# The second layer's routing: router weights as the standing operand, logits turned once, ranks from a scan and two short products

## What is computed

```python
def _L1_ffn_ref(x, w1s, w2s, w3s, W1, W2, W3, Wg):
    xf = x.reshape(-1, C)
    shared = geglu(xf, w1s, w2s, w3s)          # every token
    logits = xf @ Wg                           # 128 x 8
    idx = jnp.argmax(logits, axis=-1)          # one expert for a token
    final = jnp.zeros_like(xf)
    for e in range(N_EXPERTS):
        y = geglu(xf, W1[e], W2[e], W3[e])
        final = final + jnp.where((idx == e)[:, None], y, 0.0)
    return (shared + final).reshape(B, T, C)

x = x + 0.5 * _L0_ffn_ref(...); x = x + _L0_attn_ref(...); x = x + 0.5 * _L0_ffn_ref(...)
x = x + 0.5 * _L1_ffn_ref(_layernorm(x), ...)
x = x + _L1_attn_ref(_layernorm(x), ...)
x = x + 0.5 * _L1_ffn_ref(_layernorm(x), ...)
```

## Time and profile before

| | |
|---|---|
| median of 3 runs | 1867.86 us (1866.92 to 1868.22) |
| span of the profiled execution | 1918.1 us; the profile gives no other time of that execution |
| TensorE busy | 1729.9 us, 90% of the span |
| VectorE, ScalarE, GpSimd busy | 67%, 58%, 63% |
| granted TensorE clock, mean | 0.971 of full |

### The profile page before, as it was taken

One profiled execution on the slowest core, in us unless ns is written; L12 is line 12 of the kernel. 1 busy time (PEld: TensorE's weight loads), 2 busy tenths in 40 slices (PEclk: granted clock), 3 DMA queues, 4 the chain that ended last, 5 costly groups with the idle time before them and its releaser, 6 DMA issues. The chain is left out here.

```text
span 1918.1 us, 35727 instructions
## 1 busy us (share of the span) xinstructions
PE 1729.9 (90%) x12089; PEld 1502.7 (78%) x12089; DVE 1279.6 (67%) x2981; ACT 1105.3 (58%) x1953; POOL 1210.5 (63%) x1201
## 2 busy tenths in 40 slices
PE   7998998999999899976779988899899999988889
PEld 6887776778878688765668867777899999877777
DVE  2358988888888987889894355334576766554333
ACT  3476766667676576756655452433677777542332
POOL 4248787787868778798985243565455555444554
PEclk9999999999999999998989999999899999989999
DMA  5023433323333233232224110113544554001113
GB/s 147 1 85 104 114 100 101 95 94 105 96 110 97 86 104 108 98 89 84 94 61 118 32 37 29 45 43 104 159 130 120 148 157 124 2 33 33 42 43 104
DMA packets 121486, 166.74 MB, mean 87 GB/s; under 512 B 14710, under 2 KB 56732, under 8 KB 121308
## 3 DMA queue, kind: packets, MB, share of 16 engines
q1 hardware_dynamic: 114268, 148.86, 25.7%
q0 software_dynamic: 7040, 15.60, 2.6%
HBM read 114.20 MB, written 50.20 MB: 86 GB/s over the span
## 5 line engine op out<-in xcount | busy, mean ns | idle before, releaser
L833 POOL TENSOR_TENSOR db<-du_m,bt 128x512 f32<-128x512 f32 x256 | 329.3, 1288 | 116.7 <-DVE bank L838 115.9
L838 DVE TENSOR_TENSOR_SCAN bank<-bank,db 128x512 f32<-128x512 f32 x256 | 312.6, 1221 | 18.2 <-ACT bank L823 17.7
L864 POOL TENSOR_TENSOR y_m<-y_m,ph 128x512 f32<-128x512 f32 x240 | 312.8, 1303 | 2.0 <-DVE ph L853 2.0
L823 ACT ACTIVATE bank<-dt_m,a_neg 128x512 f32<-128x512 f32 x256 | 176.3, 689 | 85.7 <-DVE ph L853 78.9
L853 DVE TENSOR_TENSOR ph<-bank,ct 128x512 f32<-128x512 f32 x240 | 165.9, 691 | 9.4 <-POOL y_m L864 1.1
L1355 POOL TENSOR_TENSOR s_a<-s_a,mx_a 128x768 f32<-128x768 f32 x64 | 94.1, 1470 | 87.1 <-DVE mx_a L1438 87.0
L1469 PE MATMUL bank<-vb_a,pT_a 96*128 96x64 f32 x1024 | 121.7, 272 | 0.0
L1469 PEld LDWEIGHTS bank<-vb_a,pT_a 96*128 96x128 f32 x1024 | 119.8, 193 | 0.0
L375 PEld LDWEIGHTS bank<-dn,hf1b 128*128 128x128 f32 x680 | 90.2, 194 | 16.1 <-DVE x_all L437 6.8
L375 PEld LDWEIGHTS bank<-dn,hf2b 128*128 128x128 f32 x680 | 90.2, 195 | 16.0 <-DVE x_all L437 8.3
L375 PEld LDWEIGHTS bank<-dn,hf0b 128*128 128x128 f32 x688 | 90.4, 193 | 12.0 <-DVE x_all L437 2.8
(11 more groups left out here) (480 smaller groups left out, 4877.1 us busy)
## 6 DMA issues: line engine op xcount, KB each, us to landing
bt<-bc_rows SPq DMA_DIRECT2D x128, 256.0 KB, 3.4
ct<-bc_rows SPq DMA_DIRECT2D x128, 256.0 KB, 3.4
sorted<-zero_row SPq DMA_DIRECT2D x64, 288.0 KB, 4.0
k_strips_a<-k_rows SPq DMA_DIRECT2D x32, 256.0 KB, 3.0
q_strips_a<-q_rows SPq DMA_DIRECT2D x32, 256.0 KB, 4.0
q_rows<-q_hi_a SPq DMA_DIRECT2D x16, 256.0 KB, 3.0
q_rows<-q_lo_a SPq DMA_DIRECT2D x16, 256.0 KB, 3.3
k_rows<-k_hi_a SPq DMA_DIRECT2D x16, 256.0 KB, 3.2
```

Of the source, the lines that this page charges most:

```text
L823: eng.activation(DH[J % 2][:], dt[s % 2][:, j % NH, :], ACT.Exp, scale=a_neg[:, j % NH, j // NH:j // NH + 1]).then_inc(da_done.sem)
L833: eng.tensor_tensor(db[J % RD][:], du[s % 2][:, j % NH, :], bt[N % RB][:], ALU.mult).then_inc(db_done.sem)
L838: eng.tensor_tensor_scan(DH[J % 2][:], DH[J % 2][:], db[J % RD][:], 0.0, ALU.mult, ALU.add).then_inc(hs_done.sem)
L864: eng.tensor_tensor(y[s % 2][:, j % NH, :], y[s % 2][:, j % NH, :], ph[J % RP][:], ALU.add).then_inc(ys_done.sem)
```

## The change

Of the logits, the operands of the product change places. The router's weights (128 x 8, padded with zeros to 32 columns) are the standing operand, and the turned tokens of each of the four 128-token tiles pass by and write into one quarter (32 partitions) of bank `XB`. ScalarE copies the bank into `gT`, which sets `XB` free (`logits_act`), and TensorE turns it with one transpose into `YB` (`logits_pe`), from where VectorE copies the logits.

Of the ranks, VectorE forms the running count of each expert over the four tiles by a scan (`upto`) and casts the counts of the fourth (`n_all`); TensorE multiplies these 8 columns twice instead of 32, 32, 24, 16 and 8 columns; VectorE adds the result to the running counts first (`base`) and then to `upto`. A mask for the scan is made once on GpSimd. `logits_pe` stands last in slot b on TensorE, behind `ranks`; `logits_act` stands behind the GELU in slot b on ScalarE. At the program's start VectorE clears the padded weights, and the semaphores of two groups of weight loads are shared.

```diff
-        R_ACT, R_TURN, R_GATE, R_RANK, R_LOW, R_DVE = (-2, -1, -1), (-1,), (0,), (1,), (-1,), (0, 0, 1)
+        R_ACT, R_TURN, R_GATE, R_LOGITS, R_RANK, R_LOW, R_DVE = (-2, -1, -1), (-1,), (0,), (0,), (1,), (-1,), (0, 0, 1)
...
-                x = eng.matmul(XB.psum[:, k * E:(k + 1) * E], xT[q][:, k * P:(k + 1) * P], K["wg"][:], start=True, stop=True)
+                x = eng.matmul(XB.psum[k * QB:(k + 1) * QB, 0:P], K["wg"][:], xT[q][:, k * P:(k + 1) * P], start=True, stop=True)
             x.then_inc(gated.sem)
-            XB.free = (pd.sem, pd.at(s, "lg"))
+            XB.free = (gT_done.sem, gT_done.at(s))
+            yield
+
+        def logits_pe(eng, s):
+            eng.wait_ge(gT_done.sem, gT_done.at(s))
+            YB.wait(eng)
+            eng.transpose(YB.psum[:, 0:P], gT[:], C["ident"][:]).then_inc(turned.sem)
+            YB.free = (pd.sem, pd.at(s, "lg"))
             yield
 
         def rank_pe(eng, s):
-            eng.wait_ge(pd.sem, pd.at(s, "ohr"))
+            eng.wait_ge(pd.sem, pd.at(s, "all"))
             YB.wait(eng)
-            x = eng.matmul(YB.psum[:, 0:NT * E], K["tri"][:], ohr[:].rearrange("p k e -> p (k e)"), start=True, stop=False, skip_group_check=True)
-            for k in range(NT):
-                x = eng.matmul(YB.psum[:, (k + 1) * E:(NT + 1) * E], K["one_r"][:], ohr[:, k:k + 1, :].to_broadcast([P, NT - k, E]), start=False, stop=k == NT - 1, skip_group_check=True)
-            x.then_inc(ranked.sem)
+            eng.matmul(YB.psum[:, 0:E], K["tri"][:], n_all[:], start=True, stop=True)
+            eng.matmul(YB.psum[:, E:2 * E], K["one_r"][:], n_all[:], start=True, stop=True).then_inc(ranked.sem)
             YB.free = (pd.sem, pd.at(s, "run"))
...
+        def logits_act(eng, s):
+            if s >= 1:
+                eng.wait_ge(turned.sem, turned.at(s - 1))
+            eng.wait_ge(gated.sem, gated.at(s))
+            eng.copy(gT[:], XB.psum[:, 0:P]).then_inc(gT_done.sem)
+            yield
...
-            eng.wait_ge(gated.sem, gated.at(s))
-            eng.tensor_copy(lg[:], XB.psum[:, 0:NT * E].rearrange("p (k e) -> p k e", e=E)).then_inc(pd.sem)
+            eng.wait_ge(turned.sem, turned.at(s))
+            eng.tensor_copy(lg[:], YB.psum[:, 0:P].rearrange("p (k e) -> p k e", e=QB)[:, :, 0:E]).then_inc(pd.sem)
             eng.wait_ge(pd.sem, pd.at(s, "lg"))
             eng.reduce_max(mx[:], lg[:], AX.X).then_inc(pd.sem)
             eng.wait_ge(pd.sem, pd.at(s, "max"))
@@ -1901,22 +1920,26 @@
             eng.wait_ge(pd.sem, pd.at(s, "v1"))
             eng.tensor_tensor(wt[:], wide(v1), pow2, ALU.is_ge).then_inc(pd.sem)
             eng.wait_ge(pd.sem, pd.at(s, "st"))
-            eng.tensor_copy(oh[:, :, 0:1], wt[:, :, 0:1]).then_inc(pd.sem)
-            eng.tensor_tensor(oh[:, :, 1:E], wt[:, :, 1:E], wt[:, :, 0:E - 1], ALU.subtract).then_inc(pd.sem)
+            by_expert = oh[:].rearrange("p e k -> p k e")
+            eng.tensor_copy(by_expert[:, :, 0:1], wt[:, :, 0:1]).then_inc(pd.sem)
+            eng.tensor_tensor(by_expert[:, :, 1:E], wt[:, :, 1:E], wt[:, :, 0:E - 1], ALU.subtract).then_inc(pd.sem)
             eng.wait_ge(pd.sem, pd.at(s, "oh"))
-            eng.tensor_copy(ohr[:], oh[:]).then_inc(pd.sem)
+            eng.tensor_tensor_scan(upto[:].rearrange("p e k -> p (e k)"), K["not_first"][:].rearrange("p e k -> p (e k)"), oh[:].rearrange("p e k -> p (e k)"), 0.0, ALU.mult, ALU.add).then_inc(pd.sem)
+            eng.wait_ge(pd.sem, pd.at(s, "upto"))
+            eng.tensor_copy(n_all[:], upto[:, :, NT - 1]).then_inc(pd.sem)
             yield
             eng.wait_ge(ranked.sem, ranked.at(s))
             old, new = (run[s % 2], run[(s + 1) % 2]) if s else (K["cap"], run[1])
-            R8 = YB.psum[:, 0:(NT + 1) * E].rearrange("p (k e) -> p k e", e=E)
-            eng.tensor_tensor(wt[:], R8[:, 0:NT, :], old[:, None, :].to_broadcast([P, NT, E]), ALU.add).then_inc(pd.sem)
+            eng.tensor_tensor(base[:], YB.psum[:, 0:E], old[:], ALU.add).then_inc(pd.sem)
+            eng.wait_ge(pd.sem, pd.at(s, "base"))
+            eng.tensor_tensor(wt[:], upto[:].rearrange("p e k -> p k e"), base[:, None, :].to_broadcast([P, NT, E]), ALU.add).then_inc(pd.sem)
             eng.wait_ge(pd.sem, pd.at(s, "row"))
-            eng.tensor_tensor(wt[:], wt[:], oh[:], ALU.mult).then_inc(pd.sem)
+            eng.tensor_tensor(wt[:], wt[:], oh[:].rearrange("p e k -> p k e"), ALU.mult).then_inc(pd.sem)
             eng.wait_ge(pd.sem, pd.at(s, "own"))
             eng.reduce_sum(slot_f[:], wt[:], AX.X).then_inc(pd.sem)
-            eng.tensor_tensor(new[:], R8[:, NT, :], old[:], ALU.add).then_inc(pd.sem)
+            eng.tensor_tensor(new[:], YB.psum[:, E:2 * E], old[:], ALU.add).then_inc(pd.sem)
             eng.wait_ge(pd.sem, pd.at(s, "run"))
-            eng.tensor_copy(slot[:, tokens_at(s)], slot_f[:]).then_inc(pd.sem)
+            eng.tensor_scalar(slot[:, tokens_at(s)], slot_f[:], -1.0, None, ALU.add).then_inc(pd.sem)
...
+            logits = prep_steps(eng, logits_pe, R_LOGITS)
...
                 ranks(v)
+                logits(v)
...
-            prep = prep_steps(eng, prep_act, R_ACT, own_from)
+            prep, logits = prep_steps(eng, prep_act, R_ACT, own_from), prep_steps(eng, logits_act, R_LOGITS)
             for v in SLOTS:
                 if v == -1 and first:
                     norms.root(eng, NSEQ - 1)
                 if 0 <= v < EJ:
                     shared_act(eng, v)
+                logits(v)
                 prep(v)
...
-        lg, ge, wt, oh = (sb(n, [P, NT, E]) for n in ("lg", "ge", "wt", "oh"))
+        lg, ge, wt, oh = sb("lg", [P, NT, E]), sb("ge", [P, NT, E]), sb("wt", [P, NT, E]), sb("oh", [P, E, NT])
+        upto, n_all, base, gT = sb("upto", [P, E, NT]), sb("n_all", [P, E], F32R), sb("base", [P, E]), sb("gT", [P, P])
         mx, v1, slot_f = (sb(n, [P, NT]) for n in ("mx", "v1", "slot_f"))
-        ohr, run = sb("ohr", [P, NT, E], F32R), ring(2, "run", [P, E])
+        run = ring(2, "run", [P, E])
```

More of the change, by code:

```diff
@@ L189, in ffn0_up @@
     W["small"], W["wg_ld"], W["b2_ld"], W["b2_zero"] = S.dma("f0_b1_loaded"), S.dma("f0_gate_loaded"), S.dma("f0_b2_loaded", 3 * NT), cleared
-    W["raw_ld"] = [S.dma(f"f0_raw{r}_loaded", 2) for r in range(4)]
+    W["raw_ld"] = [S.dma(f"raw{r}_loaded", 2) for r in range(4)]
     W["dn_ld"] = [S.dma(f"f0_down{r}_loaded", 2) for r in range(4)]
@@ L978, in front @@
         W["raw"], W["b2_raw"] = F["spent"], F["rows"]
-        raw_ld, split = [S.dma(f"k_raw{r}_loaded", (E + 1) * NU // 2) for r in range(4)], K["split"]
+        raw_ld, split = [S.dma(f"raw{r}_loaded", (E + 1) * NU // 2) for r in range(4)], K["split"]
         def load(eng, s):
@@ L994, in sync @@
             eng.wait_ge(*M["done"](NSEQ - 1))
-            eng.dma_start(K["wg"][:], w1["gate"]).then_inc(K["dn_ld"].sem, 16)
+            eng.wait_ge(K["wg_zero"].sem, K["wg_zero"].at(0))
+            eng.dma_start(K["wg"][:, 0:E], w1["gate"]).then_inc(K["dn_ld"].sem, 16)
             for i, e in enumerate([E] + list(range(E))):
@@ L1052, in dve @@
             eng.memset(W["wg"][:], 0.0).then_inc(W["b2_zero"].sem)
+            eng.memset(K["wg"][:], 0.0).then_inc(K["wg_zero"].sem)
             eng.memset(W["b2_raw"][0:3 * NT * E, :], 0.0).then_inc(W["b2_zero"].sem)
@@ L1653, in ffn1_kept @@
     K["norms"] = [Norms(S, C, K, at_once) for at_once in (False, True)]
-    K["made"] = S.count("k_tables", 1, ("tri_f", "mask", "tri", "one_f", "one", "cap", "ids", "s128", "no", "part", "row_no", "spare"))
+    K["wg_zero"] = S.count("k_gate_zeroed")
+    K["made"] = S.count("k_tables", 1, ("tri_f", "mask", "tri", "one_f", "one", "first", "cap", "ids", "s128", "no", "part", "row_no", "spare"))
     made = K["made"]
@@ L1673, in pool @@
         eng.tensor_copy(K["one_r"][:], K["one_f"][:, 0:1].to_broadcast([P, P])).then_inc(made.sem)
+        eng.memset(K["not_first"][:], 1.0).then_inc(made.sem)
+        eng.wait_ge(made.sem, made.at(0, "first"))
+        eng.memset(K["not_first"][:, :, 0:1], 0.0)
         numbers(eng, K["cap"][:], TOK, 0, 0)
@@ L1717, in ffn1 @@
         x_T, x_lod = S.count("f1_prep_turned", NSEQ), S.count("f1_prep_lo", NSEQ)
-        gated, ranked = S.count("f1_prep_gated", NSEQ), S.count("f1_prep_ranked", NSEQ)
-        pd = S.count("f1_prep_dve", NSEQ, ("lg", "max", "ge", "wt", "v1", "st", "o0", "oh", "ohr", "row", "own", "sum", "run", "slot"))
+        gated, turned, ranked = S.count("f1_prep_gated", NSEQ), S.count("f1_prep_logits_turned", NSEQ), S.count("f1_prep_ranked", NSEQ)
+        gT_done = S.count("f1_prep_logits_copied", NSEQ)
+        pd = S.count("f1_prep_dve", NSEQ, ("lg", "max", "ge", "wt", "v1", "st", "o0", "oh", "upto", "all", "base", "row", "own", "sum", "run", "slot"))
         sent = [S.dma(f"f1_rows{q}_sent", TILES // 4) for q in range(4)]
```

2 lines of the change are left out of this document (1 added, 1 removed).

## The result

| | before | changed |
|---|---|---|
| median, first comparison | 1867.58 us (1866.92 to 1868.22, 4 runs) | 1879.97 us (1876.88 to 1882.07, 4 runs) |
| median, second comparison, another chip | 1868.98 us (29 runs) | 1881.00 us (6 runs) |
| ratio, 95% interval | | 1.0063 (1.0049 to 1.0077); 1.0062 (1.0045 to 1.0078) |
| mean granted clock over these runs | 0.978 (29 runs) | 0.9755; 0.9745 |

The change costs 12.4 us. The forecast was +5.0, to 1872.9 with a range of 1863 to 1881, and 1879.97 lies inside it, at its upper end. One execution of all that are told of here, the twelfth of the kernel with filled gaps, took 2843.77 us at a granted clock of 0.549, and it is left out of that kernel's median.

The account below looks back on a forecast made before the run. The woven ffn1 parts hang on TensorE in most slots, and on the TensorE-ScalarE-VectorE loop where a bank must come free. Per call 5.9 - 0.6 - 2.4 - 0.4 = +2.5; two calls +5.0, median 1872.9 us, range 1863 to 1881.

Parts of the forecast that it names:

- the looped slots: Slots 1, 4 and 9 of each ffn1 call, where ranks and the logits' transpose share `YB`: together +5.9 us per call.
- the two waits that were forecast: In slots 1, 4, 9 TensorE idles about 1 us before the transpose (for `run`), about 1.3 before the gate (low half).
- The loop: Transpose waits until VectorE has read the ranks and written `run`; the next slot's products stand behind it; 2.0 us per slot.
- Slot 4: Followed from transpose to transpose: 5.87 us instead of 3.75, +2.1.
- Slot 9: VectorE's sum of a finished sequence lies between, moving the row numbers by 0.4: +2.5 us.
- Slot 1: Has no down product: 4.98 us instead of 3.67, +1.3.
- Slots 2, 5 and 10: Ranks and no gate; one-hot table ready before TensorE needs it: 2.98 us, taken as -0.8 each, -2.4 per call.
- gate 0.45: TensorE's quartered gate products charged 0.45 us, including 0.09 for the gap ahead, against 0.81 before.
- Slot 0: ScalarE frees `XB` earlier, so the turned tokens wait 0.7 us less, transpose adds 0.1: -0.6 per call.
- the clock: Rival, chance 0.11: three to five of the six looped slots bring clock falls, +5 to +8.5, 1878 to 1881 us.
- The rival of the same: Chance 0.22: two or three fewer clock falls, 1868 to 1870 us, or late hand-overs already cover part of the loop.
- the prediction's own sign of being wrong: Transpose within 0.5 us of ranks, woven parts' clock moving over 0.03, or VectorE's new steps over 0.3 us each.

Follow-up runs that it names:

- the kernel with filled gaps: Changed kernel plus unread products in TensorE's two gaps of slots 1, 4 and 9, six ahead of the gate, four ahead of the transpose; 1872.08 us, ratio 1.0012.
- the addresses': Kernel before with the change's new buffers laid out in memory but unused, no instruction changed; 1870.03 us, ratio 1.0003.
- the low half first: Changed kernel with the logits' transpose ahead of the ranks, and VectorE's low half of the next tokens ahead of the routing steps; 1868.89 us, ratio 1.0000.
- ranks alone: Changed kernel with the gate put back as before, without copy or transpose, keeping the scan and two rank products; 1874.32 us, ratio 1.0027.
- the old ranks: The low half first with ranks as before (five products, no scan); 1917.64 us, ratio 0.9982, on the chip where before takes 1920.45.

## Why the prediction was right, and where it was short

**Direction.** Slower with 0.61, and it was slower, and the looped slots are there with the two waits that were forecast. They account for 5.0 of the 12.4 us.

**The loop.** Slot 4: 5.87 forecast, 6.00 measured. Slot 9: 6.25 and 6.49. Slot 1: 4.98 and 5.05. Slots 2, 5 and 10: 2.98 and 2.95 each. Scan 0.20 and 0.22; one-hot table up to the low half 2.33 after the transpose's start and 2.38 (1120.60 to 1122.98); gate 0.45 and, with the gap ahead of it, 0.10 + 0.36. Net per call +2.5 forecast, +2.8 and +2.2 measured, with the clock at 1.00 but for one fall, which before has at the same place. The terms were sized on rows of an execution 50 us longer than the timed ones; the rows that were used, without waits, were the same in both. One reading was off: slot 5, which has no gate, was held against 3.75 us, a slot with one. At the full clock it takes 3.58, so the fall there cost 1.9 us and not 1.7.

**What I had wrong in the loop** is which of its waits matters. I priced it by the wait for `run`; taking that away gave 1.1 of 5 us in the woven parts and nothing measurable in the time. With it away, VectorE's order, table before low half, set the length: turning it round took 8.8 us more off the woven parts.

**Slot 0.** Forecast -0.6, and in the first call the slot is 0.56 us shorter than in before (3.60 against 4.16). In the last call it is 0.38.

**The mis-sized term is the clock.** It stood as a rival with a chance of 0.11, +5 to +8.5 on top of the loop, 1878 to 1881, and that is where the time lies. The range took it in, the sum did not: it took the looped slots at the full clock. The mean clock of the changed kernel is 0.9745 to 0.9755, of before 0.978; the lower level is half the upper, so the mean loses at most (0.978 - 0.975) x 1875 = 5.6 us, on a range of 4.7 to 6.6. With the loop's 5.0 and the addresses' 1 that makes 10.7 to 12.6 against 12.4. This is an estimate and a ceiling: over the first 800 us, which no change touches, the two profiles have clocks of 0.99 (changed) and 0.98 (before), and the first woven part starts at 1104.60 and 1104.64, so there a lower clock cost nothing. The same sum for the low half first, -4.9 + 4.7 + 1, gives 0.8 against the -0.1 measured.

What is not shown is the rival's mechanism, that the gaps of the looped slots bring the falls. For it speaks that filling them raised the clock and gave 8.9 us back, and that in the second profile the clock fell in slot 9 between its two gaps. Against it, ranks alone has no looped slot, the low half first has no gap over 0.72 us left in these slots of the first call, and both have the changed kernel's mean clock (0.9752, 0.9754). Both have shorter waits in other slots, and no run takes those away. By the prediction's own sign of being wrong, the clock of the woven parts moving by more than 0.03, the first profile says right (1.00 and 0.98 in both kernels) and the second wrong (0.95 and 0.93). Where the falls lie in the timed runs isn't known, so the cause of the clock's share stays open.

**The rival of the same** counted on fewer falls. The mean clock is lower, not higher.

**A version better than both.** The low half first is 12.1 us under the changed kernel of its own comparison (1881.00) and level with before, 1.0000 (0.9983 to 1.0017), though its woven parts are 4.9 us shorter. Its mean clock is 0.9754 where before has 0.978: what it gained in the woven parts, it seems to have paid elsewhere, but where its falls lie in the timed runs isn't known; its profile (span 1863.4) has a fall of 13.7 us at 1322 and two short ones behind it. With the old ranks it was 0.18% faster on the chip where before takes 1920 us, at the edge of its interval. Filling what gaps it has wasn't tried.

## What to carry to other kernels

When a change makes TensorE wait in short gaps that come again and again, price the gap for itself, and look at the mean clock of the timed runs beside it: here 5 us of waits came with a slowdown of 12, and dummy products in the gaps took 8.9 back. That the gaps cause the lower clock isn't shown, since two versions without the gaps of these slots had it too. When a bank or a value passes through three engines, look at the order on the engine in the middle: one line moved on VectorE gave back more than removing the wait that the timeline names, on top of which it was done. Check that the profile at hand fits the timed runs before using its waits; here durations carried over and some waits did not. And take two profiles of each kernel before reading a few us out of a stretch of 150: with the instructions of before, two of them gave 140.6 and 143.4.

## What was not expected of the hardware

The same program took 1868.6 to 1869.3 us on three chips and 1920.45 on a fourth, and the fourth's ratios don't carry over: there a wait more gave 0.9975. Laying out buffers that nobody uses changed products of 512 columns from 390 to 395 ns, with no instruction changed. Sixty products that nobody reads, in gaps, made the changed kernel faster, 1872.08 us against 1881.00 (on another chip), at a mean clock of 0.980 against 0.9745. Falls of the clock in the woven parts differed between two profiles with the same waits, in before as in the changed kernel.
